# Flamingo block on one core: the first half's router chain cut into pieces over attention groups 10 to 28, and both output halves ahead of the values matmuls in the last four groups

## The reference, cut to what matters

```python
# C: _L1_xattn_ref, h = layernorm(x)
q = rmsnorm(h @ Wq, gq); k = rmsnorm(ctx @ Wk, gk); v = ctx @ Wv
attn = softmax(q @ k.T / sqrt(128))
x = x + tanh(g_xattn[1]) * (attn @ v @ Wo)
# D: _L1_ffn_ref, h = layernorm(x) again, 1024 tokens
logits = h @ gate_w.T                      # 64 experts
topv, topi = top_k(logits, 8); rw = softmax(topv)
W = zeros(N, E).at[arange(N)[:, None], topi].set(rw)
gu = einsum('nh,eih->nei', h, gu_w); gate, up = halves of gu
out = einsum('nei,ehi->nh', silu(gate) * up * W[:, :, None], dp_w)
out = out + sigmoid(h @ sh_gate1_w.T) * shared_expert(h)
x = x + tanh(g_ffn[1]) * out
```

## Time and profile before

| | |
|---|---|
| median of 3 runs | 687.95 us (686.17 to 687.98) |
| the profiled execution, its own time | 687.63 us |
| its span, first to last instruction | 685.8 us |
| outside the span | 1.8 us |
| mean granted TensorE clock | 0.969 of full speed |
| stage C, from `scores(1)` to `scores(31)` | 115.94 us to 377.37 us |

### The profile page before, as it was taken

The page is one execution under the profiler, slowest core; times in us unless marked ns, Lnnn a source line. Parts: engine busy times, 40 slices in busy tenths (PEclk is TensorE's granted clock), DMA queues, the critical chain, the costliest instruction groups (busy, mean ns, idle before and its releaser), DMA issues.

```text
span 685.8 us, 11757 instructions
## 1 busy us (share of the span) xinstructions
PE 622.6 (91%) x3652; PEld 526.8 (77%) x3652; DVE 491.4 (72%) x1179; ACT 428.6 (62%) x1083; POOL 211.5 (31%) x200
## 2 busy tenths in 40 slices
PE   5726767999999999999998989989999999999997
PEld 3613457899999999899897867868888788888885
DVE  3899864767777778868867468777777577777774
ACT  4838756998888888778897534444444344444441
POOL 1437243675566666545567101000000000000000
PEclk9959788999999999999999999999999999999999
DMA  8310010212000000000004044445454346455530
GB/s 306 110 47 0 1 46 1 71 47 93 3 0 3 1 1 1 2 1 1 1 9 131 4 128 142 148 117 162 153 153 158 111 139 189 162 153 153 153 92 32
DMA packets 24723, 55.33 MB, mean 81 GB/s; under 512 B 4064, under 2 KB 4704, under 8 KB 24544
## 3 DMA queue, kind: packets, MB, share of 16 engines
q1 hardware_dynamic: 24672, 54.71, 25.6%
HBM read 53.39 MB, written 1.31 MB: 80 GB/s over the span
## 4 chain that ended last, share of the span: by engine, by line
PE 72%; DVE 10%; ACT 5%; issue 3%; POOL 2%; DVEq 0%; ACTq 0%; POOLq 0%
PE bank L265 21%; PE bank L267 20%; PE bank L266 20%; PE bank L671 3%; PE bank L651 2%; ACT att L1079 2%; PE bank L643 2%; PE bank L603 1%; DVE prod L1582 1%; PE bank L706 1%; DVE rowmax L1502 1%; DVE inter L1598 1%; PE bank L591 1%; DVE stats L1275 1%; DVE o_lo L1529 1%
## 5 line engine op out<-in xcount | busy, mean ns | idle before, releaser
L1112 ACT ACTIVATE inter_hi<-inter 128x512 fp32r<-128x512 f32 (+1 forms) x66 | 41.7, 632 | 153.7 <-DVE inter L1598 149.0
L265 PE MATMUL bank<-xnT_hi,front_hi 128*128 128x512 f32 x256 | 101.8, 398 | 4.3 <-DVE front_lo L1576 2.5
L267 PE MATMUL bank<-xnT_hi,front_lo 128*128 128x512 f32 x256 | 101.9, 398 | 0.0
L266 PE MATMUL bank<-xnT_lo,front_hi 128*128 128x512 f32 x256 | 101.0, 394 | 0.0
L1602 DVE TENSOR_TENSOR inter_lo<-inter,inter_hi 128x512 fp32r<-128x512 f32 (+1 forms) x66 | 46.1, 698 | 49.4 <-ACT inter_hi L1112 49.4
L1079 ACT ACTIVATE att<-bank,shift,rq 128x256 f32<-128x256 f32 x128 | 71.2, 570 | 2.8 <-DVE shift L1509 2.8
L436 POOL TENSOR_TENSOR att<-att,rowinv 128x512 f32<-128x512 f32 x64 | 65.8, 1048 | 15.7 <-DVE rowinv L1519 15.6
L1502 DVE TENSOR_REDUCE rowmax<-bank 128x2 f32<-128x512 f32 x64 | 43.8, 686 | 36.0 <-PE bank L267 35.9
L420 POOL TENSOR_TENSOR rk<-msq,minus_half 128x4 f32<-128x4 f32 x32 | 32.4, 1012 | 107.0 <-DVE msq L1491 106.9
L1582 DVE TENSOR_TENSOR prod<-gate_s,bank 128x512 f32<-128x512 f32 (+1 forms) x66 | 45.2, 685 | 27.5 <-PE bank L267 22.4
L265 PEld LDWEIGHTS bank<-xnT_hi,front_hi 128*128 128x128 f32 x256 | 48.1, 188 | 16.4 <-DVE front_lo L1576 2.9
(11 more groups left out here) (248 smaller groups left out, 1811.9 us busy)
## 6 DMA issues: line engine op xcount, KB each, us to landing
w_all<-w_rows SPq DMA_DIRECT2D x128, 128.0 KB, 2.9
raw<-in_expert_w SPq DMA_DIRECT2D x32, 384.0 KB, 3.5
wvo_raw<-in_expert_w SPq DMA_DIRECT2D x16, 384.0 KB, 3.5
e_more<-in_expert_w SPq DMA_DIRECT2D x16, 384.0 KB, 3.5
raw<-in_head_qk SPq DMA_DIRECT2D x8, 384.0 KB, 3.2
wvo_raw<-in_head_vo SPq DMA_DIRECT2D x8, 384.0 KB, 3.1
gate_raw<-in_gate_wT SPq DMA_DIRECT2D x1, 1408.0 KB, 11.6
x<-in_x_tok SPq DMA_DIRECT2D x2, 512.0 KB, 6.3
```

The costliest lines, as they stand in the source:

```text
L265: pe.matmul(out, l_hi, r_hi_, start=start, stop=False, skip_group_check=True)
L266: pe.matmul(out, l_hi, r_lo_, start=False, stop=False, skip_group_check=True)
L267: return pe.matmul(out, l_lo, r_hi_, start=False, stop=stop, skip_group_check=True)
L1112: act.activation(inter_hi[0:rows, slot, :], inter[0:rows, slot, :], ACT.Copy).then_inc(a_Ihi, 1)
```

## The change

For the first half of the tokens, the router chain's work is the same, in other places of the streams:

- statistics and normalisation in two lots: tiles 0 and 1 in groups 10 and 12 (power on GpSimd in group 11), tiles 2 and 3 in groups 17 and 18. Before: all four in 17 and 18.
- `turn_rows(2, 0)` with its two copies in group 14 instead of 19; `turn_rows(2, 1)` stays in 20.
- `choose` is cut in three: `best_eight` in group 21, `shift_logits` in 22, the rest in 23. `weight_exps` moves from 23 to 24. `weights` is cut in two: `sum_weights` in 25 (its reciprocal now linked), the rest in 26. Before: all of `choose` in 21, all of `weights` in 24.
- `turn_weights` and `turn_shared`, with their copies, move from groups 26 and 27 to 27 and 28.
- in groups 28 to 31 `output(g - 1, 1)` is issued before `values(g)` instead of after it.

The second half's chain calls the same new functions back to back, where `choose` and `weights` stood.

```diff
 # gpsimd, at the end of group g
+                if g == 11:
+                    power(6, vare[:, 0:2], rstd[:, 0:2], 2)
                 if g == 17:
-                    power(6, vare[:, 0:4], rstd[:, 0:4], 4)
+                    power(7, vare[:, 2:4], rstd[:, 2:4], 2)
...
 # tensor
-                if g in (19, 20):
-                    turn_rows(2, g - 19, KBK)
+                if g in (14, 20):
+                    turn_rows(2, g // 20, KBK)
                 if g == 21:
                     router(0, KBK)
-                if g == 26:
+                if g == 27:
                     turn_weights(0, KBK)
-                if g == 27:
+                if g == 28:
                     turn_shared(0, KBK)
...
-                if g in (19, 20):
-                    pe.wait_ge(c_u, g - 10)
+                if g in (14, 20):
+                    pe.wait_ge(c_u, 9 + g // 20)
...
-                if g in (26, 27):
-                    pe.wait_ge(a_wk, g - 25)
+                if g in (27, 28):
+                    pe.wait_ge(a_wk, g - 26)
...
+                if n >= GROUPS:
+                    output(g - 1, 1)
                 values(g)
-                if g:
+                if 0 < g < GROUPS - 4:
                     output(g - 1, 1)
...
 # scalar
-                if g in (19, 20):
-                    copy_rows(2, g - 19, KBK)
-                if g == 26:
+                if g in (14, 20):
+                    copy_rows(2, g // 20, KBK)
+                if g == 27:
                     keep_rows(0, KBK)
-                if g == 27:
+                if g == 28:
                     keep_shared(0, KBK)
...
-                if g == 23:
+                if g == 24:
                     weight_exps(0)
...
 # vector: choose and weights cut up
-            def choose(half):
+            def best_eight(half):
                 dve.wait_ge(v_log, half + 1)
                 for i in range(4):
                     ins = dve.max(top8[:, i, :], logits[:, i, 0:EXPERTS])
                 link(dve, ins)
+            def shift_logits():
                 lg = logits[:, :, 0:EXPERTS]
                 dve.tensor_tensor(shifted[:, :, :], lg, top8[:, :, 0:1].broadcast_to([P, 4, EXPERTS]),
                                   ALU.subtract).then_inc(v_shift, 1)
+            def choose():
+                lg = logits[:, :, 0:EXPERTS]
                 for i in range(4):
                     ins = dve.match_replace(out=struck[:, i, :], in_to_replace=top8[:, i, :],
                                             in_values=logits[:, i, 0:EXPERTS], imm_value=LOWEST)
                 link(dve, ins)
                 link(dve, dve.tensor_tensor(chosen[:, :, :], struck[:, :, :], lg, ALU.not_equal))
-            def weights(half):
+            def sum_weights(half):
                 dve.wait_ge(a_wexp, 2 * half + 2)
                 link(dve, dve.tensor_tensor(chosen[:, :, :], chosen[:, :, :], wexp[:, :, :], ALU.mult))
                 link(dve, dve.tensor_reduce(wsum[:, :], chosen[:, :, :], AX.X, ALU.add))
-                dve.reciprocal(winv[:, :], wsum[:, :])
+                link(dve, dve.reciprocal(winv[:, :], wsum[:, :]))
+            def weights():
                 link(dve, dve.tensor_scalar(shg[:, :], shg[:, :], 0.5, 0.5, ALU.mult, ALU.add))
                 link(dve, dve.tensor_copy(shcat[:, :, 0].bitcast(F32R), shg[:, :]))
                 link(dve, dve.tensor_tensor(shcat[:, :, 1].bitcast(F32R), shg[:, :], shcat[:, :, 0],
                                             ALU.subtract))
                 dve.tensor_tensor(chosen[:, :, :], chosen[:, :, :],
                                   winv[:, :].unsqueeze(2).broadcast_to([P, 4, EXPERTS]), ALU.mult).then_inc(v_wt, 1)
...
-                if g == 17:
-                    dve.wait_ge(v_Y, 2)
-                    tile_stats(0, 4)
-                    ask_rstd(0, 4)
-                if g == 18:
+                if g in (10, 17):
+                    dve.wait_ge(v_Y, 1 + g // 17)
+                    tile_stats(g // 17 * 2, g // 17 * 2 + 2)
+                    ask_rstd(g // 17 * 2, g // 17 * 2 + 2)
+                if g in (12, 18):
                     ask_pow()
-                    normalise(0, 4)
+                    normalise(g // 18 * 2, g // 18 * 2 + 2)
                 if g == 21:
-                    choose(0)
-                if g == 24:
-                    weights(0)
+                    best_eight(0)
+                if g == 22:
+                    shift_logits()
+                if g == 23:
+                    choose()
+                if g == 25:
+                    sum_weights(0)
+                if g == 26:
+                    weights()
```

More of the change, by code:

```diff
@@ L470, in _ @@
                                        ALU.subtract).then_inc(g_Elo, 1)
-            power(7, vare[:, 4:8], rstd[:, 4:8], 4)
+            power(8, vare[:, 4:8], rstd[:, 4:8], 4)
             pool.wait_ge(a_rw, 3)
@@ L1639, in _ @@
                     low_m(g + 1)
-                if g in (19, 20):
-                    low_rows(2, g - 19, KBK)
+                if g in (14, 20):
+                    low_rows(2, g // 20, KBK)
                 if g == 21:
@@ L1716, in _ @@
                     take_logits(1, 2)
-                    choose(1)
+                    best_eight(1)
+                    shift_logits()
+                    choose()
                 if q == 11:
-                    weights(1)
+                    sum_weights(1)
+                    weights()
             with dve.Fori(4, EPAIRS // 4) as i:
```

## The result

| | before | changed |
|---|---|---|
| median | 687.97 us (686.17 to 689.84, 4 runs) | 679.39 us (678.99 to 682.83, 4 runs) |
| profiled execution, its own time | 687.63 us | 678.99 us |
| span | 685.8 us | 677.2 us |
| mean granted clock | 0.969 | 0.974 |

The ratio is 0.9886, with a 95% interval of 0.9844 to 0.9928: faster by 5 to 11 us.

The account below looks back on a forecast made before the run. The prediction took TensorE's own work, plus its waits for late VectorE results, to bound the kernel. Its terms, -5.26 + 1.25 - 1.67 = -5.7 us, gave 681.9, with 0.3 for the median 682.2 us; range 680.3 to 685.2.

Parts of the forecast that it names:

- What bounds the kernel: In stage C, TensorE's own work, 8.12 us an undisturbed group; disturbed groups take 9.95 us longer in all, partly waits.
- the margin at the end of a group: Between VectorE's last reciprocal and `rowmax` some 1.4 us fit free, and 0.46 us more before TensorE feels it.
- Parts 1 to 3: Through the start of group 27: statistics, normalisation, `turn_rows` -2.12 us; choice in pieces -2.69; `turn_weights` moved -0.45; sum -5.26.
- the allowances for the pieces: Costs left for moved VectorE work: 0.1 us each in groups 12 and 18, 0.05 for the choice piece coming near.
- Part 4: `weights` at the end of group 26 is held by GpSimd's `att` pair; TensorE waits 0.65, lateness reaches `turn(29, 1)`: +1.25 us.
- Part 5: Output before values: 0 in groups 28 and 30, -0.71 in 29, -0.71 and -0.25 in 31; sum -1.67 us.
- Sum: Whole kernel: -5.26 + 1.25 - 1.67 = -5.7 us.
- (b): Pieces at group ends still hit GpSimd: four or five of seven hold `rowmax` 0.7 us each, +3.1, 685.3 us; chance 0.15.
- (c): The gain is given back behind the loop, time near 687 us; chance 0.09.
- (d): Slower: each linked piece waits out both `att` operations and the power, 12.6 us over seven groups, 694.5 us; chance 0.06.

Follow-up runs that it names:

- Experiment 5: Changed kernel with the three small operations of `weights` in group 26 moved between the two `row_inverse(27)`, the product staying at the end: 678.97 us, ratio 0.9882.
- output-only kernel: Kernel before with only the swap of output and values in groups 28 to 31: 685.09 us, ratio 0.9982.
- router-only: Changed kernel with the swap of the output halves undone, leaving the router chain in pieces alone: 682.9 us, ratio 0.9943.
- experiment 9: Changed kernel with `shift_logits` and `choose` both at the end of group 22, nothing in 23: 681.78 us in one execution.
- experiments 7 and 8: Changed kernel with VectorE's `low_e(2)` put ahead of `times_up(1, 1)`: 677.45 us; the same plus Experiment 5's edit and GpSimd's second `e_lo` moved to group 29: 676.62 us.

## Why the prediction was right, and where it was wrong

- **What bounds the kernel, the margin at the end of a group**: right. Every wait that was to go has gone; groups 12, 18, 23 and 25 cost nothing visible, where 0.1 each or 0.05 was left.
- **Parts 1 to 3**: -5.26 forecast, -5.50 measured from group 14 to 26; mis-sized are the allowances for the pieces, too careful by 0.2.
- **Part 4, `weights` on GpSimd's pair**: right in place and size. TensorE waits 0.51 (0.65), group 27 takes 9.24 (9.2), the cast is held (0.96), and the lateness arrives at `turn(29, 1)` as 1.05 (1.25). Experiment 5 shows that it is this and that it passes through.
- **Part 5, output ahead of values**: right. Nothing in group 28, 0.7 in group 29 (the output-only kernel), the rest behind: -1.67 forecast, and the router-only kernel against the changed one shows 1.5.
- **Sum**: -5.7 forecast, -6.0 measured from `scores(1)` to the end, in two pairs of profiles.
- **The failed step** is the one from the sum to the median: "The runs' median is 0.3 above the profiled execution, so 682.2", and with it a range whose ends were made only of bounds of the change. The 0.3 itself held (0.4 in the changed kernel). What had no term is that one execution differs from the next with the same instructions. The profiled executions are 8.6 us apart: 6.0 of these are the change, 0.3 more than forecast, and 2.6 are the front, which the sum took at nothing. In the two profiles compared above the front differs where TensorE's granted clock does, after 98 us; over the eleven profiles on record `scores(1)` starts anywhere from 113.24 to 116.79 us, and behind stage C a fall of the clock is worth 1.2 to 1.4 us more. The 24 runs of before spread over 6.3 us, and its first three (686.17 to 687.98) already over 1.8. Six further runs of the changed kernel have a median of 682.55, 0.35 above the forecast, and all ten together one of 682.3. Beside the two sets before stood at 687.97 and 687.34, so it is the four that were a fast draw. That the front came early in all the fast ones is argued from the one that was profiled and not shown: their mean granted clocks do not set the slow one (682.83 us at 0.972) apart from the fast ones (679.00 at 0.971).
- **Rivals**: (b) needed 0.7 for each of four or five pieces; the windows show none. (c), a gain given back behind the loop, did not occur. (d) fell with the windows of groups 19, 25 and 26, as long as an undisturbed one.

## What to carry to other kernels

Before cutting a chain into pieces, find on the helper engine the gap that every iteration has, and what the neighbour engine does in it: here 1.4 us free and 0.46 more, but under GpSimd's two long operations, so that statistics, maxima and strike-outs cost their length there, while a tensor_scalar, a cast or a subtraction of two SBUF operands costs up to one GpSimd operation, however small it is. Fill a wait with work that is due anyway only where the wait's end does not hang on another engine: of four swapped halves two paid. And when a profile of each kernel is compared, align both just ahead of the first instruction that differs (here `scores(1)`, since groups 0 to 9 are alike too); what lies ahead of it is not the change's. Before a range is given, measure how far one kernel's own runs spread: here it was as far as the change.

## What the runs showed of the hardware

- Four-element operations of VectorE (tensor_scalar, cast, a subtraction of two SBUF operands) took 0.50, 0.96 and 0.96 us under GpSimd's multiplications and 0.15, 0.18 and 0.16 beside its power. The Trainium skill ("SBUF — State Buffer", "Who interferes with whom") names cast and tensor_scalar in a two-port mode, and a tensor_tensor with both inputs in SBUF, as operations that contend with GpSimd, one side blocking the other. The trace agrees, now for the cast too. GpSimd's power of 128x4 (1.0 us in the profile) held nobody visibly: the product of 128x256 took 0.43 under it.
- VectorE can also win: the comparison of experiment 9 (0.43) made GpSimd's pair of multiplications 0.24 longer (2.46 against 2.22), and the shifted logits alone 0.18 (2.22 against 2.04).
- The granted clock at 101 to 107 us, in front of stage C, was 0.99 or 1.00 in six of the eleven profiles, 0.50 in two and 0.69 to 0.72 in three, with the same instructions. Between the two profiles of one kernel it went with 2.2 us (changed) and 2.6 us (before) at `scores(1)`.
- Behind a TensorE wait of 2.5 us the clock fell to 0.50 in three of nine profiles, worth 1.2 to 1.4 us. Without that wait (experiments 7 and 8) the part behind `scores(31)` took 304.99 and 305.44 us and the clock did not fall; but it did not fall in six of the nine with the wait either, so two profiles do not show that the wait is what makes it fall.
